# Edge sort of a two-layer graph kernel: the codes stored column by column

## The reference

```python
# layer 0
msgs = edge_val[:, None] * node_features[edge_src]
agg = segment_sum(msgs, edge_dst, num_segments=N_NODES)
gnn0 = relu(agg @ W + b)
# layer 1: row = src, col = dst
e = h_l[row] + h_r[col]; e = where(e > 0, e, ALPHA * e)
ex = exp(e - segment_max(e, row)[row])
att = ex / (segment_sum(ex, row)[row] + 1e-16)
gnn1 = segment_sum(att[:, :, None] * h[col], row)
```

## Time and profile before

| | |
|---|---|
| median of 3 runs | 4306.62 us (4291.44 to 4314.83) |
| profiled execution | 4298.71 us; its span 4297.0 us |
| busy share of the span | PE 67%, DVE 62%, POOL 54%, ACT 23% |
| mean granted clock of TensorE | 0.779 |

### The profile page before, as it was taken

One profiled execution on the slowest core, in us unless ns is written; L12 is line 12 of the kernel. 1 busy time (PEld: TensorE's weight loads), 2 busy tenths in 40 slices (PEclk: granted clock), 3 DMA queues, 4 the chain that ended last, 5 costly groups with the idle time before them and its releaser, 6 DMA issues. The chain is left out here.

```text
span 4297.0 us, 46245 instructions
## 1 busy us (share of the span) xinstructions
PE 2891.0 (67%) x12954; PEld 2092.4 (49%) x12954; DVE 2664.2 (62%) x6067; ACT 970.2 (23%) x2628; POOL 2312.0 (54%) x2155
## 2 busy tenths in 40 slices
PE   3456777589999963284665556655656545799986
PEld 2334434355555543163554444434434434699952
DVE  4435898688788784546655556655656576544436
ACT  4565000000000012012321111111111123333332
POOL 0256777766666634254157777777777720365510
PEclk7777887789999875587777677777777765799975
DMA  3322333322232221364123333333333353222233
GB/s 116 83 81 86 88 88 89 91 80 86 83 87 86 83 61 50 71 149 103 62 69 94 92 92 91 92 93 93 93 93 91 92 104 120 74 72 70 72 90 120
DMA packets 203997, 379.28 MB, mean 88 GB/s; under 512 B 48927, under 2 KB 131874, under 8 KB 203620
## 3 DMA queue, kind: packets, MB, share of 16 engines
q0 software_dynamic: 102192, 279.12, 24.1%
q1 hardware_dynamic: 101556, 97.19, 7.3%
HBM read 314.12 MB, written 62.05 MB: 88 GB/s over the span
## 5 line engine op out<-in xcount | busy, mean ns | idle before, releaser
L516 POOL DMA_INDIRECT arena<-h_table,arena x1712 | 1867.0, 1091 | 926.0 <-issue 487.7
L530 DVE TENSOR_TENSOR arena<-arena,ps 128x260 f32 (+1 forms) x1712 | 720.8, 421 | 789.6 <-remote 306.0
L2131 PE MATMUL ps<-arena 128*128 128x260 f32 x1760 | 603.8, 492 | 241.1 <-issue 117.7
L1174 PE MATMUL ps<-arena 128*128 128x256 f32 x1664 | 550.3, 447 | 226.1 <-DVE arena L530 113.5
L2131 PEld LDWEIGHTS ps<-arena 128*128 128x128 f32 x1760 | 394.6, 242 | 359.4 <-issue 236.4
L1174 PEld LDWEIGHTS ps<-arena 128*128 128x128 f32 x1664 | 334.4, 221 | 392.9 <-issue 220.7
L1099 PE MATMUL ps<-arena 128*128 128x224 f16 x784 | 293.9, 528 | 49.5 <-DVE arena L942 48.1
L2113 PE MATMUL ps<-arena 128*128 x880 | 126.0, 188 | 267.3 <-ACT arena L1976 154.3
L843 DVE TENSOR_SCALAR arena<-arena 128x128 f32<-128x128 f32 x832 | 289.2, 348 | 0.4 <-DVE arena L857 0.2
L2058 DVE TENSOR_TENSOR arena<-arena 128x1024 f32<-128x1024 f32 x220 | 268.3, 1220 | 2.1 <-ACT arena L1984 2.1
L2457 POOL DMA_INDIRECT arena<-xn_table,arena x114 | 124.4, 1091 | 250.1 <-POOLq L2188 213.9
(11 more groups left out here) (516 smaller groups left out, 4535.5 us busy)
## 6 DMA issues: line engine op xcount, KB each, us to landing
arena<-h_table,arena POOLq DMA_INDIRECT x1712
arena<-in_L_ffn_w SPq DMA_DIRECT2D x32, 512.0 KB, 7.3
xn_table<-arena SPq DMA_DIRECT2D x14, 896.0 KB
slot_out<-arena SPq DMA_DIRECT2D x21, 512.0 KB
arena<-y_rows SPq DMA_DIRECT2D x12, 896.0 KB, 9.3
h_table<-arena SPq DMA_DIRECT2D x7, 924.0 KB
h_table<-arena SPq DMA_DIRECT2D x7, 896.0 KB, 4.1
arena<-in_x SPq DMA_DIRECT2D x48, 128.0 KB
```

The source lines that it names most:

```text
L516: pool.indirect_dma_start(slot[:, 0:width], None, table, bass.IndirectOffsetOnAxis(ap=idx, axis=0)).then_inc(done, 16)
L530: dve.tensor_tensor(to, to, bank(b, width), ALU.add).then_inc(gnn_add, 1)
L1174: pe.matmul(bank(n % V0_BANKS, D), hot_w[:, g % 2, u, :], rows[:, n % RING, :], start=True, stop=True).then_inc(gnn_ps, 1)
L2131: pe.matmul(bank(4 + u % GNN1_BANKS, ACC_W), hot[:, b, u, :], rows[r][:, u, 0:ACC_W], start=True, stop=True).then_inc(gnn_ps, 1)
```

## The change

The buffer of the codes is laid out [c, k, n] in place of [k, n, c]: the 224 codes of one column lie side by side, and the same code of the next column lies 224 f16 elements on. DVE's multiply goes over its operands in the same order as before, through a rearranged view, so that it writes each run of seven with a step of 224 elements; PE reads each column's 224 codes with a step of one, where it was seven. Sizes, counts, semaphores and all other operations stay.

```diff
-        codes = [take(SLOTS_S * GS).bitcast(F16).rearrange("p (k n c) -> p k n c", k=2, c=GS) for _ in range(2)]
+        codes = [take(SLOTS_S * GS).bitcast(F16).rearrange("p (c k n) -> p c k n", c=GS, k=2) for _ in range(2)]
...
-                        dve.tensor_tensor(codes[sg % 2], slots_.unsqueeze(1).to_broadcast([P, 2, SLOTS_S, GS]),
+                        dve.tensor_tensor(codes[sg % 2].rearrange("p c k n -> p k n c"), slots_.unsqueeze(1).to_broadcast([P, 2, SLOTS_S, GS]),
                                           code_16[:, :, at].unsqueeze(2).to_broadcast([P, 2, SLOTS_S, GS]), ALU.mult
                                           ).then_inc(sort_in, 1)
...
                         last = pe.matmul(bank(5, 2 * SLOTS_S), hot_pos[sg % 2][:, :, c],
-                                         codes[sg % 2].rearrange("p k n c -> p (k n) c")[:, :, c],
+                                         codes[sg % 2][:, c, :, :].rearrange("p k n -> p (k n)"),
                                          start=(n == 0 and c == 0), stop=(n == PER_PART - 1 and c == GS - 1),
```

## The result

The changed kernel takes 4964 us (median of 4 runs, 4952 to 4972) where the kernel before takes 4300 (its median over four runs, where the three first gave the 4306.62 above): a ratio of 1.154 (95% interval 1.151 to 1.158), 664 us more. The direction was forecast, the size was not: 4410 us, range 4330 to 4515. Measured again beside other kernels the ratio is 1.152 (1.150 to 1.155).

The account below looks back on a forecast made before the run. PE and DVE hold each other in the sort stage, PE nearest to a bound; DVE becomes the bound: 4.78 + 1.87 = 6.65 us, at 96% full 6.93 a group, +0.93 x 112 = +104 us: 4410 us, range 4330 to 4515.

Parts of the forecast that it names:

- The bound before, TensorE's side: Sort stage: PE nearest to a bound, 93% busy; strided read slows the seven matmuls; side by side saves 1.5 us a group.
- the 0.132 that I took as a floor: Sort matmuls: the strided weight loads, 0.132 us each, taken as the least spacing between matmuls.
- the 1.2 to 1.8 given: Sort matmuls: range of PE's saving, at least 1.2 and at most 1.8 us a group.
- I take 2.96, as L286 is the nearest: DVE's codes multiply L942: scattered writes cost 1.79 ns an element, raising it from 1.09 to 2.96 us, +1.87 a group.
- the upper end of 3.18 us: L942: dearest write price within the main forecast, from L809's step of 1.93 ns.
- a dearer scatter: Rival: L942's two-byte writes cost 2.5 ns each, L942 4.07 us, +234 us, 4540 us in all; chance 0.07.
- The plain rate: Rival: L942's writes cost only 1.04 ns an element, 1.78 us; -33 us, 4274 us in all; chance 0.15.
- How full DVE gets: Sort stage: DVE, as the new bound, runs 96% full, against 91% where it does the ranking.
- What is hidden: PE's saving: Sort stage: once DVE sets the pace, PE's saving only turns into waits for L942.
- The slack of 2.8 us: Sort stage: some 2.8 us of PE slack a group would cover a falling PE clock.
- DVE's waits for L1174: Sign: DVE's waits for the visits' matmuls, 68 us in 500 before, nearly gone; wrong if they stay.
- not near 1660: Sign: the sort's last matmul would come near 1660 us.

Follow-up runs that it names:

- TensorE's half alone: Kernel before, with only PE's read of 224 codes made side by side, DVE writing in the old order (other codes multiplied): ratio 0.987, 53 us less.
- The form by itself: The changed L942's multiply run alone, in a kernel that leaves out the whole computation: 7.63 us.
- The single operations: Two kernels that leave out the computation and run only single operations with nothing beside them; the form before and the changed one among them, the latter 7.63 us.
- L942 = 2.58 us: Changed kernel with DVE's loops reordered, slots innermost, so it writes side by side and reads 14 bytes apart: ratio 1.0075.
- PE's half taken back: Changed kernel, with PE reading with a step of seven as before (other codes multiplied): ratio 1.179, against 1.154 with both halves.
- the clock held up: Changed kernel with 40 products of zeros on PE before it waits for a group's codes: ratio 1.138, 4900 us, against 4959 without on the same chip.

## Why the prediction was right in direction and wrong in size

**The bound before, TensorE's side.** The mechanism was right. The read of 14-byte steps was the cost; side by side the seven take 0.90 us at granted clock 1.00, starting 0.107 us apart, below the 0.132 that I took as a floor (the load's own duration is no floor; loads overlap). With TensorE's half alone that saves 1.7 us a group, within the 1.2 to 1.8 given. In the changed kernel, at clock 0.50 after each long wait, it saves 2.63 - 1.51 = 1.1, just under the range.

**The price of the write.** The step that failed: "I take 2.96, as L286 is the nearest." The term was +1.87 us a group and measured +6.54, 4.77 ns an element against 1.79. The mechanism, a toll for writes that scatter, is the one at work; the toll that I took, from f32 rows, is 2.7 times too small for f16, where each write fills half a word. The rows for the bound, L286 and L809, were both f32 writes, and the text said that no row had an f16 write with a long step; the upper end of 3.18 us then rested on f32 as well. The rival "a dearer scatter" was right in kind, with 2.5 ns and a chance of 0.07, far too low on both counts. The form by itself takes 7.635 us, so nothing else is in it.

**The plain rate.** The rival took L942 at the plain rate of 1.04 ns, 1.78 us. The Trainium skill ("VectorE: DVE Perf Modes", Side-by-side: where the cycles go for N=2048 bf16) gives a two-tensor operation two results a cycle only for 16-bit data with step one, and otherwise one. The single operations agree where the output lies side by side (1.79 us with an operand repeated along the inner run). For this write the measured time is more than four times as long: how fast the engine makes results says nothing of what the writes cost.

**How full DVE gets.** I took 96%. At L942 = 2.58 us it was 96.7; at 7.63 us 92.8, and with TensorE's half alone 86. From L942's start to the next instruction's it is 7.22 us in the timeline above, where it was 1.00: 6.22 more. With that the sum gives (4.78 + 6.22)/0.96 = 11.46 us a group, +611 us, 4918; with the measured 92.8% for 96 it gives 11.85, +655, 4962 us. So of the 554 us that the forecast missed, the write's price accounts for about 507, and most of the rest is that DVE ran less full.

**"What is hidden: PE's saving."** Wrong. It was worth 1.0 us a group, because PE can be only two visits ahead of the codes: the longer L942 is, the more of PE's work comes after it, at the slow clock. The slack of 2.8 us was an average over the group; it lay before the codes, not behind them. The two ends are measured (PE's half taken back, and the clock held up); that the order of PE's work is the reason is read from the code and the timeline.

**The rest.** As forecast: neighbours unchanged, PE's waits for L942 longer, nothing lost outside the stage. Not as forecast: DVE's waits for L1174 are not nearly gone, which the prediction itself had named as a sign of being wrong. They fell from 68 to 32 us in 500, but 500 us held 83 groups and now hold 42: 0.82 and 0.77 us a group. PE is 47% busy and not 60, and the last sort matmul comes at 2218.7 us and not near 1660: both follow from the longer write.

## What to carry to other kernels

When a layout is turned so that one engine reads side by side, price the engine that now writes: by lines of 16 bytes touched, and by whether it fills 4-byte words. If the data are two bytes wide, turn them in pairs, or swap the loops so that the stride falls on a read. And when the trace has a similar row of another width, its price may be only a lower bound, as it was here: f32 rows for an f16 write.

## What the runs showed of the hardware

- A write that comes to a new 16-byte line costs 1.7 to 1.8 ns in whole words and 4.2 to 5.0 ns in half words, in all multiplies tried on DVE, in its copy from PSUM and on ACT (7.67 us for 1568 f16, 448 bytes apart). DVE's copy within SBUF pays about half of either, 0.87 and 2.40 ns. A read costs 1.77 ns a line. PE's doesn't follow PE's clock: columns 14 bytes apart start a matmul every 0.350 us at granted clock 1.00 and every 0.350 us at 0.50, (5.08 - 0.529)/13.
- Fours of f16 neighbours 448 bytes apart cost no more than side by side: 975 against 954 ns.
- A gather that POOL starts while L942 runs nearly always lasts until it ends. Of 121 gathers that started during one in the changed kernel, 112 ended 0.24 to 0.29 us after it, having taken up to 7.87 us; the other nine had started within 0.04 us of L942's own start and took 0.94 to 0.96 us, the median outside it. It didn't set the pace here: no wait of PE for a gather stands in the stage.
- Idle time of PE can have a price on the engines behind it: 40 useless matmuls a group made the changed kernel 60 us faster, with the mean granted clock from 1000 to 1500 us at 0.88 in place of 0.66.
